# A Perceiver layer on one core: where the value steps stand in the quads that hold a wide stage

## The reference, cut to what matters

```python
x = x + xattn(layernorm(x), ctx, ctx)      # Q, K, V projections; per head:
#   dot = Q @ K.T / 4;  out = softmax(dot) @ V;  out @ Wh.T + bh
x = x + attn(layernorm(x))                 # feat = exp(clip(xn @ omega * c - s)), causal
#   products of query and key features (per 128 rows), times V, divided by a sum
x = x + ffn(layernorm(x))                  # (silu(x @ Wg.T) * (x @ Wu.T)) @ Wd.T
```

## Time and profile before

| | |
|---|---|
| median of 3 runs | 915.33 us (913.16 to 915.46) |
| profiled execution, its own time | 914.84 us |
| its span | 913.1 us |
| PE busy | 844.7 us, 93% of the span |
| ACT busy | 532.0 us, 58% |
| DVE busy | 432.7 us, 47% |

### The profile page before, as it was taken

The page is one execution under the profiler, slowest core; times in us unless marked ns, Lnnn a source line. Parts: engine busy times, 40 slices in busy tenths (PEclk is TensorE's granted clock), DMA queues, the critical chain, the costliest instruction groups (busy, mean ns, idle before and its releaser), DMA issues.

```text
span 913.1 us, 20640 instructions
## 1 busy us (share of the span) xinstructions
PE 844.7 (93%) x8815; PEld 573.3 (63%) x8815; DVE 432.7 (47%) x796; ACT 532.0 (58%) x578; POOL 48.3 (5%) x76
## 2 busy tenths in 40 slices
PE   6799999999999999999899999999999999978776
PEld 4566666666566666666566666666566666646555
DVE  6532235355744446535744446534744445214653
ACT  2167777676577666656577666657577666840101
POOL 1033000000000000000000000000000000000000
PEclk9899999999999999999999999999999999998799
DMA  5757564465333333336343333336334333001000
GB/s 178 236 182 246 207 206 163 147 202 174 127 140 139 139 139 133 107 135 183 128 139 139 139 140 114 116 136 191 117 139 140 139 117 116 1 24 24 1 1 15
DMA packets 58738, 120.09 MB, mean 132 GB/s; under 512 B 21521, under 2 KB 29713, under 8 KB 55121
## 3 DMA queue, kind: packets, MB, share of 16 engines
q1 hardware_dynamic: 56848, 114.31, 36.8%
q0 software_dynamic: 1792, 4.40, 1.6%
HBM read 78.84 MB, written 37.75 MB: 128 GB/s over the span
## 4 chain that ended last, share of the span: by engine, by line
PE 75%; DVE 10%; issue 6%; ACT 4%; DVEq 2%; DMA 1%; POOL 1%; SPq 0%; POOLq 0%; ACTq 0%
PE ps_o L750 23%; PE ps_s L762 16%; PE ps_pa L594 10%; PE ps_pa L555 10%; ACT probs L1026 3%; PE ps_pa L720 2%; PE ps_pa L695 2%; PE ps_pa L707 2%; PE ps_pa L686 1%; PE ps_pa L616 1%; PE ps_pa L643 1%; PE ps_pa L699 1%; DVE feat L1264 1%; DVE feat L1248 1%; DVE ss L1250 1%
## 5 line engine op out<-in xcount | busy, mean ns | idle before, releaser
L1026 ACT ACTIVATE probs<-ps_s 128x1024 f32<-128x1024 f32 x512 | 495.9, 1023 | 272.0 <-PE ps_s L762 243.1
L750 PE MATMUL ps_o<-probs,values 128*17 128x256 f32 x4096 | 258.1, 382 | 0.0
L762 PEld LDWEIGHTS ps_s<-qstack,kstack 64*128 64x128 f32 x2048 | 139.9, 185 | 116.9 <-issue 57.4
L762 PE MATMUL ps_s<-qstack,kstack 64*128 64x256 f32 x2048 | 196.8, 307 | 13.1 <-ACT probs L1026 12.2
L750 PEld LDWEIGHTS ps_o<-probs,values 128*17 128x17 f32 x4096 | 101.4, 97 | 99.4 <-issue 14.3
L1063 DVE TENSOR_SCALAR kparts<-ps_pa,b_heads 128x512 fp32r<-128x512 f32 x64 | 48.0, 751 | 123.8 <-PE ps_pa L555 123.8
L1080 DVE TENSOR_TENSOR values<-ps_pa,bv_pair 128x512 f32<-128x512 f32 x64 | 44.3, 692 | 109.6 <-PE ps_pa L594 109.3
L594 PE MATMUL ps_pa<-wv_hi,ctx_hi 128*128 128x256 f32 x256 | 78.3, 306 | 1.6 <-DVE wv_lo L1051 1.6
L594 PE MATMUL ps_pa<-wv_hi,ctx_lo 128*128 128x256 f32 x256 | 72.5, 283 | 0.0
L594 PE MATMUL ps_pa<-wv_lo,ctx_hi 128*128 128x256 f32 x256 | 72.5, 283 | 0.0
L555 PE MATMUL ps_pa<-ctx_hi,wk_hi 128*128 128x512 f32 x128 | 57.7, 451 | 4.5 <-DVE kparts L1065 2.3
(11 more groups left out here) (238 smaller groups left out, 798.1 us busy)
## 6 DMA issues: line engine op xcount, KB each, us to landing
kstack<-kscr SPq DMA_DIRECT2D x96, 512.0 KB, 5.3
kscr<-kparts SPq DMA_DIRECT2D x64, 512.0 KB, 2.7
ctx_raw<-ctxT SPq DMA_DIRECT2D x32, 512.0 KB, 6.8
qstack<-qscr SPq DMA_DIRECT2D x12, 256.0 KB, 3.7
qscr<-qparts SPq DMA_DIRECT2D x4, 512.0 KB, 2.8
xh<-x SPq DMA_DIRECT2D x4, 256.0 KB, 6.4
kstack<-kstack SPq DMA_DIRECT2D x2, 512.0 KB, 6.3
qstack<-ksample SPq DMA_DIRECT2D x4, 256.0 KB, 4.0
```

Of the source, the lines that this page charges most:

```text
L750: last = mm(ps_o[32 * j:32 * j + DH + 1, g * S:(g + 1) * S], values[par][:, i, head_of_step(g, j), :], prob[:, j * S:(j + 1) * S], start=b ...
L762: last = mm(ps_s[s % 2][:, j * S:(j + 1) * S], kstack[par][rows, u, i * P:(i + 1) * P], queries[rows, u, :], start=True, stop=True)
L1026: nc.scalar.activation(probs[n % AHEAD][:, :], ps_s[n % 2][:, :], ACT.Exp, scale=float(DH) ** -0.5).then_inc(fast["exp_done"], 1)
```

## The change

Quads with a wide stage no longer have two value pairs. They run all value steps that are outstanding (up to n-1) together behind the first slots, and none behind the second slots. A counter, `valued`, keeps how far the value steps have come. The first quad of a chunk without a wide stage keeps its two groups, and plain quads are as they were. So in each batch the value steps of 12 quads, which stood in 24 pairs, stand in one pair and 11 groups of four, and the two left over join the first group of the quad behind them, at step 80. No instruction is added or taken away, and only PE's order changes.

```diff
--- before.py
+++ after.py
@@ -796,6 +796,14 @@
                     pe.wait_ge(fast["operand"], fast.at("operand", tail_of(b - 1), "o"))
                 value_product(fast, n, s, q % 2, q % NCH == 0, q % NCH == NCH - 1, q * TT + s // G)
 
+            valued = [0]
+
+            def values_up_to(n):
+
+                while valued[0] < n:
+                    fast_values(valued[0])
+                    valued[0] += 1
+
             def fast_slot(b, p, s):
 
                 q = b * NCH + p
@@ -840,23 +848,20 @@
                     pe.wait_ge(fast["k_stacked"][p % 2], (q // 2 + 1) * STACKED)
                     for s in range(0, STEPS, QUAD):
                         n = q * STEPS + s
-                        halves = s == 0 or any(name in WIDE for t in range(QUAD)
-                                               for name, _ in stages_at(b, p * STEPS + s + t))
+                        wide = any(name in WIDE for t in range(QUAD) for name, _ in stages_at(b, p * STEPS + s + t))
                         for t in (0, 1):
                             fast_scores(b, q, s + t)
                         for t in (0, 1):
                             fast_slot(b, p, s + t)
-                        if halves and n:
-                            for t in (0, 1):
-                                fast_values(n - LAG + t)
+                        if wide or s == 0:
+                            values_up_to(n)
                         for t in (2, 3):
                             fast_scores(b, q, s + t)
                         for t in (2, 3):
                             fast_slot(b, p, s + t)
-                        for t in range(LAG if halves else 0, QUAD):
-                            fast_values(n - LAG + t)
-            for t in range(LAG):
-                fast_values(B * BS + t - LAG)
+                        if not wide:
+                            values_up_to(n + QUAD - LAG)
+            values_up_to(B * BS)
             products(fast, TAIL[:NORMALISED], tail_of(B - 1), True)
 
             pe.wait_ge(judged, 1)
```

## The result

The changed kernel takes 931.51 us in the median of 4 runs (930.0 to 932.09), against 915.39 for the kernel before (913.16 to 917.13). The ratio is 1.0171, interval 1.0149 to 1.0192: slower by 1.7%. A second set of 6 runs gave 1.0174 (1.0140 to 1.0208). The profiled execution took 930.0 us, its span is 928.2. In the changed file the lines behind the edit stand five further down: L1026 is now L1031, L1264 is L1269, L1268 is L1273; L762 and L750 are the same.

The account below looks back on a forecast made before the run. PE's own sequence was taken as the bound, with ACT's pace making nearly all the loss. Terms summed to 4.53 us a batch, 13.6 for three; added to the profiled 914.84 they gave 928.4 us, range 921 to 935.

Parts of the forecast that it names:

- The 2.97 us of two score pairs: From one score pair's start to the first work behind the next pair: 2.97 us, set by ACT's exponentials and two tiles.
- A stages: A stages followed by a second slot: A0, A1, A3, A6 lose 0.52 us each, A2 and A5 0.84 each.
- A7: A stage followed by the quad of step 80: from its scores to pv3 5.49 us instead of 5.60, -0.11.
- feat1: Stage whose follower, a key projection, waits for DVE's clip: 6.73 us instead of 5.96, +0.77.
- feat3: Stage followed by A4, 3.29 us from its scores; to the value projection behind, 6.66 us instead of 6.85, -0.19.
- Merging: Four value steps together take 1.85 us against 1.98 for two pairs; 36 boundaries removed gain at most 4.7 us.
- Value projections in a second slot, three in a batch: Each loses 0.23 us waiting for the first pair's eviction and wins 0.13 by merging: +0.10 each, +0.30 a batch.
- feat2: Its added ACT exponential was costed at nothing, since pv0 and a value projection's 12 matmuls precede the next scores.
- The chain of value step, exponential and score step: Rival: exponentials behind the first of four value steps exceed their 0.41 us cover by 0.27 at 33 groups; 937 us, chance 0.05.
- The granted clock: Rival: short PE gaps throttle the clock, one half-speed stretch a batch adding 12 us in all; 940 us, chance 0.03.
- Only the bank waits count: Rival: exponentials keep up, so A stages hold the next slot only until the bank frees at 2.51 us; 919 us, chance 0.07.
- Faster: Rival: each removed boundary between slot matmuls and a value pair saves more, for example 0.75 us; 906 us, chance 0.04.

Follow-up runs that it names:

- half_exp_after: Changed kernel with each cross-attention exponential over 512 of 1024 columns; 0.9848 of the kernel before, where the kernel before with the same cut had 0.9814.
- defer_six: Kernel before, with the second value pair left out only in the quads of A0, A1, A2, A3, A5 and A6; ratio 1.0114 to the kernel before.
- defer_32: Kernel before, with the second value pair left out only in the quad at step 32; ratio 1.0077 to the kernel before, 1.0028 when run again.
- late_feat0: Changed kernel with ACT taking feat0's exponential behind that of step 35 instead of step 33; ratio 1.0176 to the kernel before, 1.0169 when run again.

## Why the prediction was right, and where it was short

- **What bounds.** Right: PE's busy time did not change, and each wait added its length.
- **The 2.97 us of two score pairs.** Right to 0.01 at A0, and half_exp_after shows that it is ACT's pace: with short exponentials the slot comes at 2.54, the bank's 2.51.
- **A stages.** The cycle of A0, from its scores to those of A1: 273.29 to 279.71 is 6.42, where 2.97 + 1.59 + 1.85 makes 6.41. defer_six measured the six at 3.80 against 3.76.
- **A7, feat1, feat3.** 5.48 against 5.49; 266.55 to 273.29 is 6.74 against 6.73; A4 starts 3.24 behind the scores against 3.29, and the value projection behind it 6.68 against 6.66.
- **Merging.** A group of four is 1.85 apart from what follows, as in the earlier trace rows. The Trainium skill (TensorEngine Tiling (Array Packing), Tiling Modes, Key Properties) says that changing the tiling mode drains the engine. In the trace a removed boundary brings the 0.13 us of the sum and no more: the slot ahead of the group of four takes 1.60 (276.26 to 277.86), as the 1.59 ahead of a pair.
- **The step that was mis-sized** is "Value projections in a second slot, three in a batch, ... +0.10 each, +0.30". At the first of them, behind feat0, ACT was late with step 34's exponential, and the place cost 0.88 us a batch (6.57 to 7.45, and defer_32 alone). late_feat0 takes this back to 0.05. With +0.88 in place of +0.10 the sum is 5.3 us a batch and 15.9 in all, against 16.1 from the timelines. I had looked for this cause at feat2 and not at feat0, and the bounds of the terms had no room for this place.
- **Where the time was lucky.** 928.4 us is 1.6 from the profiled execution's 930.0, but the effect was missed by 2.5 us, 13.6 against 16.1. The changed kernel's execution reached step 128 2.44 us earlier than the other with the same instructions, and lost 1.5 behind the stretches. Neither is the change's: two executions of one kernel (defer_32 and defer_32_again) differ by 2.4 us in the first and by 1.6 in the last part. By the medians the loss is 16.1 (931.51 less 915.39), and the first wide stretch grew by 5.4 us and not by 4.5.
- **The rivals.** The chain of value step, exponential and score step fits: the scores behind the groups of four wait for nothing (273.29, 279.71). The granted clock was 1.00 in the three wide stretches of the profiled execution (256 to 344, 468 to 560 and 679 to 765 us), with PE busy for 81.47 of 88 us in the first. *Only the bank waits count* fails at the tile waits and at defer_six, 3.31 us a batch where the bank alone gave 1.0. *Faster* fails with the boundaries: 0.13 us each.

## What to carry to other kernels

Count, for each pair of instructions that share a tile, the work that stands between the first's end and the second's start, and compare it with what the reader of the tile takes; joining two groups of matmuls moves that cover from one place to another, and its own gain here, 0.13 us a join, is small beside the 0.97 us that PE then lost at an A stage. Do this for every place of a kind with the reader's own queue in view, since the one place that differed was the one where another instruction stood ahead on ACT. Read the loss from the starts of the matmuls, since the idle time in the brackets was 0.65 us where the place lost 0.97. Where a wait is removed, ask which other one it was hiding.

## What the runs showed of the hardware

PE's wait for the landing of `y` changes from run to run (none, 0.98, 1.24 and 2.08 us in the kernels with whole exponentials), and once the clock fell with it. Busy time in three stretches of the second execution of the changed kernel (columns as in the earlier trace rows, then the share of the DMA engines and GB/s):

```profile
225.00:228.00 3.00, 0.92 (x10) 0.74 (x11) 0.00 (x0) 1.94 (x2) 0.00 (x0) 0.92 0.93 297
228.00:231.00 3.00, 3.00 (x10) 2.52 (x9) 0.69 (x1) 0.00 (x0) 0.00 (x0) 0.51 0.17 64
231.00:234.00 3.00, 3.00 (x28) 2.15 (x31) 2.60 (x4) 0.58 (x1) 0.00 (x0) 1.00 0.09 35
```

In the first stretch PE had waited 2.08 us for the landing and was busy for 0.92 us of 3. In the next the granted clock is 0.51, near 1.2 GHz, though PE is busy for all 3 us of it, and the third has it full again. That execution's batch 1 took 55.07 us from step 0 to step 32 where the others (with the exponential uncut) took 51.4 to 51.6. The wait of 1.24 us in late_feat0 left the clock at 1.00. The 3.6 us between the executions, some 1.5 more than the wait itself, are 0.4% of a run, more than the differences that the last experiments looked for.
